# Slots of the split parts used in turn, third values stored ahead of the stack loads, first norms by batch with a square root on ScalarE, routing sums on GpSimd

## The reference, cut to what matters

```python
x = x + tanh(g_xattn[0]) * attention(layernorm(x), ctx, ctx, ...)     # layer 0
x = x + tanh(g_ffn[0])   * experts(layernorm(x), expert_indices, ...)
x = x + tanh(g_xattn[1]) * attention(layernorm(x), ctx, ctx, ...)     # layer 1
x = x + tanh(g_ffn[1])   * quantised_ffn(layernorm(x), ...)
```

## Time and profile before

| | |
|---|---|
| times of three runs | 956.46, 958.40, 959.63 us (median 958.4) |
| the profiled execution | 958.25 us, of which the span from first to last instruction 956.4 us |
| busy | PE 860.7 us (90%), DVE 634.4 (66%), ACT 497.3 (52%), POOL 154.4 (16%) |
| mean granted TensorE clock | 0.957 |
| issue of a pair of slots' DMAs to landing | 3.1 us (median of 64) |
| issue of a store of values to landing | 5.1 us (median of 8) |

### The profile page before, as it was taken

The page is one execution under the profiler, slowest core; times in us unless marked ns, Lnnn a source line. Parts: engine busy times, 40 slices in busy tenths (PEclk is TensorE's granted clock), DMA queues, the critical chain, the costliest instruction groups (busy, mean ns, idle before and its releaser), DMA issues. The chain is left out here.

```text
span 956.4 us, 13634 instructions
## 1 busy us (share of the span) xinstructions
PE 860.7 (90%) x4064; PEld 434.0 (45%) x4065; DVE 634.4 (66%) x1286; ACT 497.3 (52%) x659; POOL 154.4 (16%) x263
## 2 busy tenths in 40 slices
PE   6879999999986999999998799999999979993098
PEld 3532333333353666666665333333333554441087
DVE  5969888888771222222348888888887478688932
ACT  1426777777741111111114467777777684597650
POOL 1223011111164000000025133100004404000000
PEclk9999999999997999999999899999999989997589
DMA  8586856664455111110147793333320000000011
GB/s 250 173 219 141 211 123 168 167 166 134 134 176 171 34 33 33 33 32 28 33 134 233 205 241 82 77 81 78 79 58 2 1 1 0 1 0 0 0 39 50
DMA packets 71325, 91.38 MB, mean 96 GB/s; under 512 B 26086, under 2 KB 56934, under 8 KB 71270
## 3 DMA queue, kind: packets, MB, share of 16 engines
q1 hardware_dynamic: 63564, 67.96, 28.0%
q0 software_dynamic: 5584, 19.93, 6.2%
q10 hardware_dynamic: 2128, 2.89, 0.9%
HBM read 62.90 MB, written 27.44 MB: 94 GB/s over the span
## 5 line engine op out<-in xcount | busy, mean ns | idle before, releaser
L1337 DVE TENSOR_REDUCE MX<-PS 128x1 f32<-128x512 f32 x512 | 320.7, 682 | 44.0 <-PE PS L1796 43.0
L940 ACT ACTIVATE Pt<-PS 128x1024 f32<-128x1024 f32 x256 | 248.3, 1021 | 102.4 <-PE PS L1817 102.4
L1796 PE MATMUL PS<-KSt,BIG 96*128 96x512 bf16 x512 | 176.2, 388 | 14.7 <-DVE BIG L1253 10.4
L1817 PE MATMUL PS<-BIG,KSt 99*128 99x512 bf16 x512 | 151.0, 381 | 0.2 <-DMA BIG<-MR 0.2
L1828 PE MATMUL PS<-Pt,VS 128*17 128x512 f32 x1024 | 136.1, 598 | 0.0
L1796 PEld LDWEIGHTS PS<-KSt,BIG 96*128 96x128 bf16 x512 | 40.7, 97 | 160.3 <-DVE MX L1337 99.0
L1971 PE MATMUL PS<-BIG,KSt 128*128 x184 | 85.2, 607 | 0.7 <-DVE KSt L1463 0.4
L1993 PE MATMUL PS<-BIG,Pt 128*128 x368 | 84.2, 382 | 1.1 <-DVE Pt L1458 1.1
L1458 DVE COPY Pt<-PS 128x512 f32<-128x512 f32 x46 | 29.7, 686 | 81.8 <-PE PS L1982 81.8
L2059 PE MATMUL PS<-KSt,BIG 128*128 128x512 f32 x192 | 83.2, 593 | 0.7 <-ACT BIG L1042 0.7
L1817 PEld LDWEIGHTS PS<-BIG,KSt 99*128 99x128 bf16 x512 | 49.9, 98 | 53.4 <-ACT Pt L940 2.4
(11 more groups left out here) (199 smaller groups left out, 1029.9 us busy)
## 6 DMA issues: line engine op xcount, KB each, us to landing
qk_parts<-BIG SPq DMA_DIRECT2D x64, 192.0 KB, 3.1
BIG<-in_w POOLq DMA_DIRECT2D x12, 1024.0 KB, 5.9
BIG<-qk_parts SPq DMA_DIRECT2D x32, 192.0 KB, 3.3
KSt<-qk_parts SPq DMA_DIRECT2D x32, 192.0 KB, 3.8
v_rows<-BIG SPq DMA_DIRECT2D x8, 544.0 KB, 5.1
VS<-v_rows SPq DMA_DIRECT2D x32, 136.0 KB, 3.0
BIG<-qk_parts SPq DMA_DIRECT2D x32, 128.0 KB, 3.9
KSt<-qk_parts SPq DMA_DIRECT2D x32, 128.0 KB, 4.0
```

Of the source, the lines that this page charges most:

```text
L940: act.activation(PP[:, 2 * (kc % 2) + half, :, :].rearrange("p h t -> p (h t)"), ST[half], ACT.Exp, scale=DK ** -0.5).then_inc(exp_done, 1)
L1337: dve.tensor_reduce(MX[:, g % 2, i % TB, i // TB:i // TB + 1], ring(i), AX.X, ALU.max, negate=True).then_inc(max_taken, 1)
L1796: pe.matmul(ring(i), QS[0:ROWS, g, h, qc * P:(qc + 1) * P], KS[0:ROWS, g, h, :], start=True, stop=True).then_inc(max_done, 1)
L1817: last = pe.matmul(ST[half][:, i * S:(i + 1) * S], KS[0:ROWS + PARTS, g, h, kc * P:(kc + 1) * P], QS[0:ROWS + PARTS, g, h, :], start=True, ...
```

## The change

- Slots: `TURN` gives each of k0, k1, q0, k2, q1, k3, q2, q3 the pair A and B in turn. k1 goes to pair B; all later ones again follow, in their slot, the one two places before them.
- SP: `store_values(layer, 2)` is issued before the first `load_stack`, which waits for pair A alone.
- DVE's first norms come in three sets (4, 4 and 8 tiles), with `norm_var` and `norm_rstd` (reciprocal, two tensor_tensor, tensor_scalar, reciprocal) around a Sqrt on ACT (`norm`), instead of `root_norm`.
- The routing sums go to POOL (`route_tiles`, `route_upto`), into groups 0 and 3 of layer 0's first attention batch; `route_ranks` moves behind `take_values(0, 0)`, and PE's `count_slots` behind the first values.
- Layer 1: the low parts of q0 go from DVE to POOL, behind the 16 gathers; the rests of q1 move behind `root_norm("back")`.
- PE begins with 14 matmuls of ones into bank 7 (`keep_busy`).

```diff
+        TURN = {("k", 0): (0, 0), ("k", 1): (1, 0), ("q", 0): (0, 1), ("k", 2): (1, 1),
+                ("q", 1): (0, 2), ("k", 3): (1, 2), ("q", 2): (0, 3), ("q", 3): (1, 3)}
         def slot(kind, p, c):
-            return c if kind == "k" or p == B - 1 else KC + c
+            return KC * TURN[kind, p][0] + c
         def landed(layer, kind, p):
-            return 32 * (((B + 1) * layer + (B if kind == "q" else p)) if slot(kind, p, 0) == 0 else (B - 1) * layer + p)
+            return 32 * (B * layer + TURN[kind, p][1])
...
                 store_parts(layer, "k", 2)
+                store_values(layer, 2)
                 for c in range(KC):
-                    sp.wait_ge(part_out[slot("k", 0, c)], landed(layer, "k", 1))
                     sp.wait_ge(part_out[slot("q", 0, c)], landed(layer, "q", 1))
                 load_stack(layer, 0, 0)
-                store_values(layer, 2)
                 load_stack(layer, 0, 1)
...
# GpSimd
                     for i in range(ROUTED):
                         gather(i)
+                    low_parts(1, "q", 0)
...
+            def route_tiles():
+                steps = 0
+                gp.wait_ge(ranks_taken, 1)
+                gp.memset(before[:, 0, :], 0.0).then_inc(tile_sums, 1)
+                for i in range(1, ROUTED):
...
+                elif g == 0:
+                    route_tiles()
+                elif g == 3:
+                    route_upto()
# ScalarE
             def prep(layer):
+                if layer == 0:
+                    norm("first0")
                 act.wait_ge(ab_in, AB_IN[layer])
                 two_parts(layer, "k", 0)
+                if layer == 0:
+                    norm("first1")
                 two_parts(layer, "k", 1)
                 copy_xnt(layer, 0)
                 two_parts(layer, "q", 0)
                 if layer == 0:
+                    norm("first2")
                     act.wait_ge(gates_in, 16)
                     act.activation(tg[:, :], gates[:, :], ACT.Tanh).then_inc(tg_ready, 1)
# VectorE
                 rests(0, "k", 0)
-                root_norm("first0")
+                link(dve, norm_rstd("first0"))
+                norm_writes("first0", 0, 0, NORM_TILES["first0"])
                 take_values(0, 0)
-                norm_writes("first0", 0, 0, NORM_TILES["first0"])
+                route_ranks()
+                link(dve, norm_stats(NORM_TILES["first1"], "first1"))
+                norm_var("first1")
                 rests(0, "k", 1)
+                link(dve, norm_rstd("first1"))
                 take_values(0, 1)
-                link(dve, norm_stats(NORM_TILES["first1"], "first1"))
+                norm_writes("first1", 0, 1, NORM_TILES["first1"])
+                link(dve, norm_stats(NORM_TILES["first2"], "first2"))
+                norm_var("first2")
                 rests(0, "q", 0)
-                root_norm("first1")
                 rests(0, "k", 2)
+                link(dve, norm_rstd("first2"))
                 take_values(0, 2)
-                norm_writes("first1", 0, 2, NORM_TILES["first1"])
+                norm_writes("first2", 0, 2, NORM_TILES["first2"])
                 rests(0, "q", 1)
...
                 rests(1, "q", 0)
-                low_parts(1, "q", 0)
...
-                rests(1, "q", 1)
                 root_norm("back")
                 dve.scalar_tensor_tensor(shift[:, 0:ROUTED], ...).then_inc(back_shift, 1)
+                rests(1, "q", 1)
                 take_values(1, 3)
...
             route_slots()
-            route_ranks()
-            norm_stats(range(TB), "first0")
-            route_tiles()
-            link(dve, norm_stats(range(TB, 2 * TB), "first0"))
+            link(dve, norm_stats(NORM_TILES["first0"], "first0"))
+            norm_var("first0")
# TensorE
+            def keep_busy(count, to):
+                for _ in range(count):
+                    pe.matmul(to, ones[:, :], ones[:, :], start=True, stop=True)
...
+            pe.wait_ge(gp_consts, 3)
+            keep_busy(14, bank(7)[:, 0:P])
             prep(0)
```

More of the change, by code:

```diff
@@ L474, in x_tile @@
             return TB * ORDER[layer][i // TB] + i % TB
-        NORMS = [("first0", range(2 * TB)), ("first1", range(2 * TB, NT)), *[(f"moe{h}", range(2 * h, 2 * h + 2)) for h in range(TB)], ("rest", range(ROUTED, NT)), ("back", range(ROUTED)),
+        NORMS = [("first0", range(TB)), ("first1", range(TB, 2 * TB)), ("first2", range(2 * TB, NT)), *[(f"moe{h}", range(2 * h, 2 * h + 2)) for h in range(TB)], ("rest", range(ROUTED, NT)), ("back", range(ROUTED)),
                  ("ffn_a", x_tiles(FFN_A)), ("ffn_b", x_tiles(FFN_B))]
-        NORM_NO = {"ffn_a": 0, "ffn_b": 1}
+        NORM_NO = {"first0": 0, "first1": 1, "first2": 2, "ffn_a": 3, "ffn_b": 4}
         NORM_TILES = dict(NORMS)
@@ L587, in attention @@
             def attention(layer):
-                for c in range(KC):
-                    sp.wait_ge(part_out[c], 32 * (B + 1) * (layer + 1))
-                    sp.wait_ge(part_out[KC + c], 32 * (B - 1) * (layer + 1))
+                for j in range(2 * KC):
+                    sp.wait_ge(part_out[j], 32 * B * (layer + 1))
                 sp.wait_ge(v_out, 16 * B * (layer + 1))
@@ L749, in split_max, with route_upto @@
                 gp.tensor_tensor(MP[:, :, 2, :], MD[:, :, :], MP[:, :, 1, :], ALU.subtract).then_inc(max_parts, 1)
+            def route_tiles():
[3 more added lines that the diff above has]
+                for i in range(1, ROUTED):
+                    steps += 1
+                    gp.wait_ge(tile_sums, steps)
+                    gp.tensor_tensor(before[:, i, :], before[:, i - 1, :], totals[:, i - 1, :], ALU.add).then_inc(tile_sums, 1)
+                gp.wait_ge(tile_sums, ROUTED)
+                gp.tensor_tensor(rt[0][:, :], before[:, ROUTED - 1, :], totals[:, ROUTED - 1, :], ALU.add).then_inc(tile_sums, 1)
+                gp.wait_ge(tile_sums, ROUTED + 1)
+                gp.tensor_scalar(rt[1][:, :], rt[0][:, :], 1.0 / P, (P - 1) / (2.0 * P), ALU.mult, ALU.add).then_inc(tile_sums, 1)
+                gp.wait_ge(tile_sums, ROUTED + 2)
+                gp.tensor_scalar(rt[1][:, :], rt[1][:, :], MAGIC, 1.0, ALU.add, ALU.mult).then_inc(tile_sums, 1)
+                gp.wait_ge(tile_sums, ROUTED + 3)
+                gp.tensor_scalar(rt[1][:, :], rt[1][:, :], -MAGIC, 1.0, ALU.add, ALU.mult).then_inc(tile_sums, 1)
+            def route_upto():
+                gp.wait_ge(tile_sums, ROUTED + 4)
+                gp.tensor_copy(upto[:, 0:1], rt[1][:, 0:1]).then_inc(tile_sums, 1)
+                for e in range(1, E):
+                    gp.wait_ge(tile_sums, ROUTED + 4 + e)
+                    gp.tensor_tensor(upto[:, e:e + 1], upto[:, e - 1:e], rt[1][:, e:e + 1], ALU.add).then_inc(tile_sums, 1)
             def attention(layer, between):
@@ L769, in load_experts @@
                     load_w1(NG * (n - 1) + g)
+                elif g == 0:
+                    route_tiles()
+                elif g == 3:
+                    route_upto()
                 elif g == 2:
                     gp.wait_ge(ab_in, AB_IN[0])
-                    for c in range(KC):
-                        gp.wait_ge(part_out[c], 32 * (B + 1))
-                        gp.wait_ge(part_out[KC + c], 32 * (B - 1))
+                    for j in range(2 * KC):
+                        gp.wait_ge(part_out[j], 32 * B)
                     gp.wait_ge(v_out, 16 * B)
@@ L1109, in route_ranks @@
                                 bank(0)[:, 0:ROUTED * E]).then_inc(ranks_taken, 1)
[L1111 to L1123, removed]
             def route_places():
+                dve.wait_ge(tile_sums, ROUTED + 4 + E)
                 link(dve, dve.tensor_tensor(rt[2][:, :], upto[:, :], rt[1][:, :], ALU.subtract))
@@ L1149, in norm_stats @@
                 for i in tiles:
-                    if name in ("first0", "first1") and i % TB == 0:
+                    if name in ("first0", "first1", "first2") and i % TB == 0:
                         dve.wait_ge(x_in[i // TB], 16)
@@ L1663, in prep @@
                 n0 = B * layer
-                if layer == 0:
-                    count_slots()
                 pe.wait_ge(awk_in, 16 * (layer + 1))
@@ L1670, in prep @@
                 project_values(layer, 0)
+                if layer == 0:
+                    count_slots()
                 pe.wait_ge(ct_in[ORDER[layer][1]], 16 * (layer + 1))
```

2 lines of the change are left out of this document (1 added, 1 removed).

## The result

The changed kernel takes 950.68 us (median of 8 executions, 947.59 to 953.78) against 956.14 us of the kernel before (8, 954.79 to 959.63, on the same chip): a ratio of 0.9938, 95% interval 0.9922 to 0.9954, so 4.4 to 7.5 us faster where 2.8 were forecast, and just under the range. The profiled execution of after took 947.59 us (span 945.9), the fastest of its eight; that of before, 958.25, lies above the median of its kernel here. The two profiles therefore differ by 10.5 us, where the medians differ by 5.5.

The account below looks back on a forecast made before the run. PE, busy 90% of the span, was taken to lose time in one large hole ending each layer's preparation. Gains of 1.2 and 1.6 us, 2.8 off 958.25, gave 955.45, set at 955.6 us against the median; range 951.0 to 959.6.

Parts of the forecast that it names:

- the sum: Gains at PE's two restarts added up: 1.2 us in layer 0 and 1.6 in layer 1, 2.8 us in all.
- the restart: PE resuming after its large idle time at each preparation's end; forecast at 53.9 us in layer 0, 531.6 in layer 1.
- clock rival: Layer 0: PE idle 3.1 us before q1 lowers its clock, q1 and v3 run slow, 961 us; chance 0.12.
- the walk: Step-by-step timing of layer 0's preparation, ending with PE resuming at 53.9 us, 1.2 us gained.
- one slow half: Milder case of slow q1 and v3 in layer 0, only one half at the low clock: 958.5 us.
- The table: ACT's table load before layer 0's first Sqrt: only after its wait, 1.28 us, so Sqrt ends at 14.9 us.
- The last wait: End of layer 0's preparation: group 0's six stack loads, issued from 47.0 to 49.4 us, land at 53.7 to 53.9.
- Routing on POOL: Some 20 small steps beside maxima in layer 0's attention, used three batches later: no cost taken.
- the slots in layer 0: k1's high part loses its 4.33 us store wait, but comes at 25.2 us, no earlier than the present 24.45.
- PE's 28 extra passes: Matmuls from 1.5 us to near 8 to 10 us, letting k0 run at full clock: no effect either way.
- The free port: DVE's small steps are not held beside POOL and Tanh finds its table: 7.7 us gained, 950.7 us; chance 0.20.
- The same wait in other clothes: Loads and store share queues, third values taken 3.9 us late: layer 0 gains nothing, 957 to 958.9 us; chance 0.20.

Follow-up runs that it names:

- The fills: Two timings of the kernel before with 18 matmuls of ones behind the last values of each preparation, nothing else changed: 959.43 us (ratio 0.9962) and 957.73 us (0.9953).

## Why the prediction was off

**The clock was named and not priced: this is the step that failed.** "What bounds" said that the clock is low for a while behind each hole, at 0.68, and the sum then put the price of the change as "how much earlier each restart comes". A stall that gets shorter can also leave the clock up. The price could have been read: in before the way from the restart to the first score takes 25.09 us in layer 0 and 26.52 in layer 1, two lengths for the same work, so that at least 1.4 us hung on the clock. The fills show 3.7 and 4.5 us (in the profile 1.2 and 2.8). After collects a part of it, about 2 us by its clock and by its three profiles, in some executions more than in others. The other part of the miss is the restarts, 4.1 us where 2.8 were added up. The only clock rival that I weighed was one in which it falls where it hadn't; one in which it stays up had no chance, and my last sentence, wrong "if any stretch behind the restarts has another length than now", is where the trace says so.

**That rival's mechanism came, and cost nothing.** Window of after, 40 to 47 us, and PE:

```profile
40.00:47.00 7.00, 5.55 (x7) 2.49 (x8) 6.83 (x19) 2.45 (x5) 2.27 (x2) 0.53 0.80 232
```

```profile
41.45 6.55 PE L1790 MATMUL PS<-BIG 128*128 128x512 f32 x8 [3.22 <-ACT BIG L902]
```

PE stood for 3.22 us ahead of q1 (3.1 forecast), the clock fell to 0.53, and q1 took 6.55 us. But v3 ran at full speed, q1 had started 2.0 us ahead of the walk (41.45 for 43.4), and the last values were taken at 52.26, ahead of the loads. The rival also overlooked what the slow q1 gives back: of the three executions of after, the one with the slowest q1 has the shortest idle time at the restart and the shortest way to the first score. Its time for one slow half doesn't follow from its own terms either: v3 would end at 54.4 and the last values at 55.8, 0.7 us past 55.12, and less the 1.6 of layer 1 that is 957.5, not 958.5.

**Layer 0, 2.1 us measured where 1.2 were worked out** (2.1 to 2.6 over three executions). The walk was right in its order and in its sizes, and ran late from its first number on. Timeline of after, forecast stamps in the text behind it:

```profile
5.40 1.28 ACT L876 ACT_TABLE_LOAD   x1 [5.40 <-issue]
...
13.17 0.20 ACT L876 ACTIVATE sd<-ve 128x4 f32<-128x4 f32 x1 [6.49 <-DVE ve L1190]
14.11 1.41 DVE L1254 SCALAR_TENSOR_TENSOR BIG<-PS,BQK,BIG 128x512 f32<-128x512 f32 x2 [0.97 <-ACT BIG L882]
15.61 2.27 POOL L714 TENSOR_TENSOR BIG<-BIG 128x512 bf16<-128x512 f32 x2 [12.32 <-ACT BIG L888]
15.63 1.15 DVE L1232 TENSOR_TENSOR nw<-ve,nw 128x4 f32<-128x4 f32 x1
16.82 1.08 DVE L1233 TENSOR_TENSOR nw<-nw,sd 128x4 f32<-128x4 f32 x1
17.93 0.17 DVE L1234 TENSOR_SCALAR nw<-nw 128x4 f32<-128x4 f32 x1
...
36.64 1.28 ACT L925 ACT_TABLE_LOAD   x1
```

- The table: I let ACT load it only once its wait was over, as before did at 12.12. In after the Sqrt's table is loaded at 5.40, under the wait for DVE, so Sqrt ends at 13.37, not 14.9. Nearly all of the 1.5 us by which the walk is late is this; x landed 0.27 us earlier as well.
- Rests of k0 end at 15.52 (17.05 forecast). The norm takes 2.88 us from 15.43 (2.85), its two tensor_tensor 1.15 and 1.08 beside POOL and the tensor_scalar behind them 0.17; the same three times over. The Trainium skill (SBUF — State Buffer, "SBUF: two separate sides") says that a DVE operation with two SBUF inputs waits out a whole GpSimd operation that reads SBUF, if that one began first. The trace agrees.
- Values of k0 at 21.05 (22.65), second statistics' variance 23.25 (24.95), rests of k1 25.51 (27.3), rests of q0 35.86 (37.85), the table load ahead of tanh at 36.64 with 1.28 us (as forecast), third values 44.43 (46.5): each 1.5 to 2.1 early, with the distances from one to the next right to 0.3 us. The Trainium skill (ScalarE: Activation LUTs, "What ACT_TABLE_LOAD costs") gives about 1283 ns for the load, with which the trace agrees, and some 1380 ns of a drain besides, which it doesn't show: Tanh starts at 37.93.
- The last wait: the first load is issued at 44.93 (47.0), the last at 48.26 (49.4), since the second issue lasted 1.25 us: of 2.1 us ahead, 0.9 are lost there. It isn't chance: with the new order on SP this issue lasts 1.25 to 1.45 us in every profile, and 0.42 to 0.62 where the loads go ahead of the third values. The restart is 0.9 early, 53.04 for 53.9.
- Routing on POOL at nothing, the slots in layer 0 at nothing, PE's 28 extra passes at nothing: the first stands by the trace (the sums start at 79.26, behind the first scores, and end at 82.44, and POOL then stands for 7.16 us), the second by the run with the old slots. The passes ended at 7.15 and k0 took 3.70 us; no run took them away alone.

**Layer 1, 2.0 us where 1.6 were worked out.** On before's clock time (after's plus 4.28): q0 starts at 504.57 (504.5 forecast), values of batch 1 at 505.88 (506.5), k2's second high part at 515.47 (516.6), q0's low parts on POOL until 516.93 (517.05), combine 6 takes 2.41 (2.25), statistics end at 525.14 (525.45), the norm takes 3.2 (3.2), restart 531.2 (531.6). The 0.4 us are the shorter store of values. Undone one by one the slots are worth 1.8 us and the two moves 0.5 to 0.9, and together they give 2.0.

**The other rivals.** The free port falls on two steps of 1.1 us in every norm. "The same wait in other clothes" was true of the third values, taken at 43.01 to 44.43 (41.16 before), but under the 47.8 us from which it was to decide, since DVE gained more ahead of it. It is nearly what the kernel with the old order on SP does: the restart at 54.09.

**The range** ended at 951.0, with the outer part of the free port cut off; with 2 to 4 us of clock as a case of its own it would have reached 949 or so. A part of the distance is the starting point: the forecast counted from 958.4 us, the median of three executions of before, and eight have 956.14. Counted from there the sum gives 953.3. Which side of the range's edge the time fell on is thus partly luck; that the gain is 5.5 us where 2.8 were forecast is not.

## What to carry to other kernels

The price of a stall of TensorE is its length and what the slow clock behind it costs; the second is read from the same stretch of work where it runs at either level, and a run that fills the stall with useless matmuls measures it by itself. An engine that is full in front of a hand-over (here DVE) pays back small steps taken off it, down to the next wait in line, so name that wait, and look whether an issue order alone moves it. A part of a diff can be large and bring nothing: undo the parts one by one before building on them.

## What the runs showed of the hardware

- ACT stood for 2 to 12 us in layer 1's preparation, in some executions, for something that no engine of the core released (12.02 us in one of after; 9.8 in one of before with its stalls filled; none in the first profiles of both). It explains prep 1 of 51.25 and 53.52 us, and probably a part of the spread of 951.5 to 965.7 us within twelve executions of after. What it waits for stays open.
- The placing of ACT's table load for the first function of the program: ahead of its wait in one kernel (5.40), behind it in the other (12.12), at 1.28 us in both.
- On SP, the issue of the second stack load behind a store of values took 1.25 to 1.45 us in the nine profiles with after's order, beside 0.42 to 0.6 for the other five of its group. What makes it long stays open.
- After one and the same idle time of 3.2 us ahead of q1, the granted clock from 40 to 47 us was 0.53, 0.76 and 1.00 in three executions of after: where the clock falls is not fixed by the kernel alone.
